# The sixteen transposes of K in one run, into the gram's banks, ahead of the third projection's last tile

## The reference

```
z_l = h @ W_lang.T ; z_g = h @ W_grav.T ; v = h @ W_V.T
A_l = max(zn @ zn.T, 0) * not_eye                  # zn: rows of z_l, each of unit length
A_g = exp(-max(|z_g i - z_g j|^2, 0) / (2 sigma^2)) * not_eye
K   = w_l * row_normalised(A_l * mask) + (1 - w_l) * row_normalised(A_g * mask)
x   = layernorm(x + (K @ v) @ W_O.T)
```

## Time and profile before

| | us |
|---|---|
| median of 3 runs | 1019.85 (1018.96 to 1020.45) |
| span of the profiled execution, first to last instruction | 1016.6 |
| TensorE busy | 1002.1 |
| VectorE busy | 646.2 |
| ScalarE busy | 322.4 |
| GpSimd busy | 151.8 |

### The profile page before, as it was taken

How to read it: one execution, slowest core, us unless ns; L and a number is a source line. 1 busy time by engine, 2 the same in 40 slices (tenths; PEclk the granted TensorE clock), 3 DMA queues, 4 the chain that set the end, 5 groups by cost and what they waited for, 6 DMA issues and landing times.

```text
span 1016.6 us, 15123 instructions
## 1 busy us (share of the span) xinstructions
PE 1002.1 (99%) x5194; PEld 867.0 (85%) x5194; DVE 646.2 (64%) x1786; ACT 322.4 (32%) x632; POOL 151.8 (15%) x155
## 2 busy tenths in 40 slices
PE   9999999999999999999999999999999999999997
PEld 7788888888888888888888889888898888888885
DVE  4565757657485674757757586574856748477488
ACT  4333233232422333233232332324233232242341
POOL 1202111021200212102021100212001121010231
PEclk9999999999999999999999999999999999999999
DMA  8320130403104040140401304031040401403001
GB/s 218 72 43 1 46 80 5 121 0 94 31 21 104 0 117 7 42 84 0 124 0 59 66 11 113 0 97 28 21 103 0 114 11 42 83 0 125 1 21 63
DMA packets 155378, 55.04 MB, mean 54 GB/s; under 512 B 133824, under 2 KB 137920, under 8 KB 155328
## 3 DMA queue, kind: packets, MB, share of 16 engines
q1 hardware_dynamic: 153216, 53.49, 20.9%
q10 hardware_dynamic: 2112, 1.05, 0.4%
HBM read 37.75 MB, written 16.78 MB: 54 GB/s over the span
## 4 chain that ended last, share of the span: by engine, by line
issue 66%; PE 20%; POOL 11%; DVE 2%; POOLq 0%; DMA 0%; ACT 0%; DVEq 0%
POOL mask_r L1014 6%; PE ring L283 5%; PE ring L285 5%; PE ring L284 4%; POOL rstd L1021 3%; PE g_bank L283 2%; PE g_bank L285 2%; PE g_bank L284 2%; POOL r L1008 1%; PE g_bank L278 1%; PE ring L278 1%; POOL u_odd_lo L996 1%; PE g_bank L321 0%; DMA y<-in_x_dram 0%; DVE al L823 0%
## 5 line engine op out<-in xcount | busy, mean ns | idle before, releaser
L660 DVE TENSOR_TENSOR zl_lo<-ring,zl_hi 128x512 fp32r<-128x512 f32 x64 | 44.1, 691 | 117.3 <-ACT zl_hi L525 117.3
L569 ACT ACTIVATE off<-g_bank 128x128 f32<-128x128 f32 (+1 forms) x128 | 40.4, 331 | 227.8 <-DVE diag_out L736 227.3
L1021 POOL TENSOR_TENSOR rstd<-var_eps,neg_half 128x1 f32<-128x1 f32 x64 | 46.0, 719 | 410.2 <-DVE var_eps L855 410.2
L283 PE MATMUL ring<-xT_hi,wgT_hi 128*128 128x512 f32 x256 | 101.6, 397 | 0.0
L283 PE MATMUL ring<-xT_hi,wlT_hi 128*128 128x512 f32 x256 | 101.4, 396 | 0.0
L283 PE MATMUL ring<-wvo_hi,xT_hi 128*128 128x512 f32 x256 | 101.0, 395 | 0.0
L285 PE MATMUL ring<-xT_hi,wlT_lo 128*128 128x512 f32 x256 | 99.9, 390 | 0.0
L285 PE MATMUL ring<-wvo_hi,xT_lo 128*128 128x512 f32 x256 | 99.8, 390 | 0.0
L285 PE MATMUL ring<-xT_hi,wgT_lo 128*128 128x512 f32 x256 | 99.8, 390 | 0.0
L284 PE MATMUL ring<-xT_lo,wgT_hi 128*128 128x512 f32 x256 | 99.8, 390 | 0.0
L284 PE MATMUL ring<-xT_lo,wlT_hi 128*128 128x512 f32 x256 | 99.8, 390 | 0.0
(11 more groups left out here) (121 smaller groups left out, 2248.8 us busy)
## 6 DMA issues: line engine op xcount, KB each, us to landing
xb<-in_x_dram SPq DMA_DIRECT2D x60, 256.0 KB, 4.7
out_dram<-y SPq DMA_DIRECT2D x60, 256.0 KB, 2.0
y<-in_x_dram SPq DMA_DIRECT2D x14, 1024.0 KB, 5.7
y<-in_x_dram SPq DMA_DIRECT2D x4, 256.0 KB, 5.3
al<-in_L_gnn_W_grav_dram ACTq DMA_DIRECT2D x4, 256.0 KB, 5.9
ag<-in_L_gnn_W_lang_dram SPq DMA_DIRECT2D x1, 1024.0 KB, 9.8
xb<-in_L_gnn_W_V_dram SPq DMA_DIRECT2D x1, 1024.0 KB, 11.9
mask_r<-in_L_gnn_W_O_dram SPq DMA_DIRECT2D x4, 256.0 KB, 9.1
```

What stands on the lines that cost most here:

```text
L283: nc.tensor.matmul(psum, lh, rh, start=k == 0, stop=False)
L569: nc.scalar.activation(off[:, mine[0]:mine[-1] + 1, :], g_bank[i][:, j0 * P:(j0 + len(mine)) * P] .rearrange("p (c n) -> p c n", n=P), ACT ...
L660: nc.vector.tensor_tensor(pair[1][:, i, :], bank[:, :], pair[0][:, i, :].bitcast(F32), ALU.subtract).then_inc(evacuated, 1)
L1021: nc.gpsimd.tensor_tensor(rstd[:, i:i + 1], var_eps[:, i:i + 1], neg_half[:, 0:1], ALU.pow)\
```

## The change

Inside the main loop, the four `transpose_k` calls become one, `transpose_whole_k`: sixteen transposes in a row ahead of `u` tile 3, written to the four gram banks, which the masked `zl` gram has left by then. They wait for `k_ready` row tile by row tile and for no ring bank. The four K tiles leave the ring's order, so a batch has 18 tiles in it and not 22. ACT and DVE take the four high and low parts right behind one another, from the gram banks, with three semaphores of their own (`kT_turned`, `kT_hi_written`, `kT_split`); `aggregate` waits for `kT_split`. On DVE the four `lo_k` stand between `u` tiles 2 and 3, `x_transpose(b + 2, 0)` moves from before `lo` of `u` tile 3 to behind it, and the two `lo` of K that stood between `row_sums` and `statistics` of the first two `out` tiles are gone. On ACT the two high parts of K that stood between those of the input are gone too. `last_two` keeps its order.

```diff
@@ -61,8 +32,8 @@
 
 
 BATCH = ([("zg", 1, 0), ("hsq", 0, 0), ("zg", 1, 1), ("zg", 1, 2), ("zg", 1, 3), ("zl", 1, 0), ("r", 0, 0),
-          ("zl", 1, 1), ("zl", 1, 2), ("zl", 1, 3), ("u", 1, 0), ("u", 1, 1), ("u", 1, 2), ("kT", 0, 0),
-          ("u", 1, 3), ("kT", 0, 1), ("out", 0, 0), ("kT", 0, 2), ("out", 0, 1), ("kT", 0, 3), ("out", 0, 2),
+          ("zl", 1, 1), ("zl", 1, 2), ("zl", 1, 3), ("u", 1, 0), ("u", 1, 1), ("u", 1, 2),
+          ("u", 1, 3), ("out", 0, 0), ("out", 0, 1), ("out", 0, 2),
           ("out", 0, 3)])
 
 LAST = (BATCH[:10]
@@ -71,6 +42,7 @@
            ("out", 0, 3), ("kT", 1, 1), ("out", 1, 0), ("kT", 1, 2), ("out", 1, 1), ("kT", 1, 3), ("out", 1, 2),
            ("out", 1, 3)])
 SPLIT = ("zg", "zl", "u", "kT")
+assert len(BATCH) % 2 == 0
 
 
 def splits(tiles):
@@ -200,6 +172,8 @@
         deg_step = sem("deg_step")
         DEG_G, DEG_ALL = 3, 7
 
+        kT_turned, kT_hi_written, kT_split = sem("kT_turned"), sem("kT_hi_written"), sem("kT_split")
+
         bn_written, moments, var_ready, rstd_ready, y_done = (
             sem("bn_written"), sem("moments"), sem("var_ready"), sem("rstd_ready"), sem("y_done"))
 
@@ -432,10 +406,19 @@
                     pe.wait_ge(k_ready, (self.b + db) * T + (i + 1))
                     transposed(bank, [al[:, i, j * P:(j + 1) * P] for j in range(T)]).then_inc(stream_ready, 1)
 
+                def transpose_whole_k(self):
+
+                    for i in range(T):
+                        pe.wait_ge(k_ready, self.b * T + (i + 1))
+                        transposed(g_bank[i], [al[:, i, j * P:(j + 1) * P] for j in range(T)]).then_inc(kT_turned, 1)
+
                 def aggregate(self, db, i, parity):
 
                     bank = self.begin(("out", db, i))
-                    pe.wait_ge(evacuated, self.stream.upto(("kT", db, i)))
+                    if ("kT", db, i) in self.stream.place:
+                        pe.wait_ge(evacuated, self.stream.upto(("kT", db, i)))
+                    else:
+                        pe.wait_ge(kT_split, self.b * T + (i + 1))
                     kT_i = [t[:, i, :].rearrange("p (k n) -> p k n", n=P) for t in kT]
                     product(bank[:, :], lambda k: tuple(t[:, k, :] for t in kT_i), whole_row(u[parity]))\
                         .then_inc(stream_ready, 1)
@@ -456,13 +439,10 @@
                     s.project("zl", i)
                 for i in range(3):
                     s.project("u", i)
-                s.transpose_k(0, 0)
+                s.transpose_whole_k()
                 s.project("u", 3)
-                s.transpose_k(0, 1)
                 for i in range(T):
                     s.aggregate(0, i, parity)
-                    if i + 2 < T:
-                        s.transpose_k(0, i + 2)
 
             def last_two(b, stream):
                 s = Steps(b, stream)
@@ -560,6 +540,10 @@
                     name = (kind, db, i)
                     split_hi(ring[self.stream.bank(name)], self.stream.upto(name), pair, i)
 
+                def hi_k(self, i):
+                    act.wait_ge(kT_turned, self.b * T + (i + 1))
+                    nc.scalar.activation(kT[0][:, i, :], g_bank[i][:, :], ACT.Copy).then_inc(kT_hi_written, 1)
+
                 def copy_off(self, db, diag_read, done, row_tiles=range(T)):
 
                     for i in row_tiles:
@@ -618,14 +602,12 @@
                 until_zl(s)
                 for i in range(3):
                     s.hi("u", 1, i, u[1 - parity])
-                s.hi("kT", 0, 0, kT)
+                for i in range(T):
+                    s.hi_k(i)
                 s.hi("u", 1, 3, u[1 - parity])
-                s.hi("kT", 0, 1, kT)
 
                 for k in range(T):
                     whole_hi_part(b + 2, k, xT)
-                    if k + 2 < T:
-                        s.hi("kT", 0, k + 2, kT)
 
             def last_two(b, stream):
                 s = Steps(b, stream)
@@ -728,6 +710,11 @@
                 def lo(self, kind, db, i, pair):
                     name = (kind, db, i)
                     split_lo(ring[self.stream.bank(name)], self.stream.split_upto(name), pair, i)
+
+                def lo_k(self, i):
+                    dve.wait_ge(kT_hi_written, self.rows(0, i))
+                    nc.vector.tensor_tensor(kT[1][:, i, :], g_bank[i][:, :], kT[0][:, i, :].bitcast(F32),
+                                            ALU.subtract).then_inc(kT_split, 1)
 
                 def diagonals(self, db, rows_done, factor, col, done, row_tiles=range(T)):
 
@@ -898,18 +885,16 @@
                 s.combine(0, 2)
                 s.combine(0, 3)
                 s.lo("u", 1, 2, u_next)
-                s.lo("kT", 0, 0, kT)
+                for i in range(T):
+                    s.lo_k(i)
+                s.lo("u", 1, 3, u_next)
                 x_transpose(b + 2, 0)
-                s.lo("u", 1, 3, u_next)
-                s.lo("kT", 0, 1, kT)
                 for i in range(T):
                     if i + 1 < T:
                         x_transpose(b + 2, i + 1)
                     whole_lo_part(b + 2, i, xT)
                     s.residual(0, i)
                     s.row_sums(0, i)
-                    if i + 2 < T:
-                        s.lo("kT", 0, i + 2, kT)
                     s.statistics(0, i)
                     if i:
                         s.normalise(0, i - 1)
```

## The result

The changed kernel takes 1021.30 us (median of 17 runs, 1020.63 to 1022.62) against 1019.66 for the kernel before, measured beside it (17 runs, 1018.52 to 1020.45). The ratio of the two is 1.0021, 95% interval 1.0014 to 1.0028: slower, by about as much as a measurement of this kernel can tell. The profiled execution took 1020.85, with a span of 1018.9; the span before was 1016.6.

A forecast was written before the change was run, and what follows sets the result against it. TensorE, 99% busy, bounds the kernel; at a return VectorE's last instruction of the old batch times it. Six returns x 0.56 lost minus 8 x 0.12 gained, +2.40 on 1019.85, gives 1022.25 us; its own range 1020.9 to 1024.4.

The forecast's parts named there:

- TensorE's part: K stage: one run of sixteen transposes, priced from the kernel's start, gains 0.12 us a batch; bounds nothing to 0.17.
- VectorE's part: Last `normalise`, counted from the start of the K stage: 1.33 + 0.63 - 0.60 - 0.80 = 0.56 us later; bounds 0.40 to 0.75.
- the other three terms: VectorE: `x_transpose` 0 behind `lo`, 0.63 later; second `lo` of K gone, 0.60 earlier; third and fourth gone, 0.80 earlier.
- The two small gaps that I set equal: VectorE: `whole_lo_part` 0 waits for ScalarE's copy; the wait before the first residual, 0.74 against 0.65, goes; taken to cancel.
- Where it costs: At six returns the mirror comes 0.56 us later; elsewhere nothing, third diagonal ready at 369.99 before its gram row at 370.14.
- The sum: Whole kernel: six returns lose 3.36 us, eight K stages gain 0.96, net +2.40; range +1.0 to +4.5.
- the 3.25 us between the median and the span: Added to the forecast span of 1019.0 as the median's excess over the profiled span, giving 1022.25 us.
- VectorE's lateness reached TensorE: Rival at returns: lateness does not reach TensorE, only 14 x 0.12 = 1.7 less stands, 1018.15 us; chance 0.17.
- The second stop: Rival at returns: VectorE's 1.56 us stop amid the diagonals moves, up to 9.4 us either way, 1013 or 1032; chance 0.07.
- VectorE did not catch up: Rival: VectorE catches up, its end comes a microsecond earlier, the returns' 5.2 us go, 1013.0 us; chance 0.10.
- the run did not wait for `combine`: Rival in the K stage: the last `combine` becomes late, 17 us lost, 1037; chance 0.04 together with the clock.
- the clock stayed at 1.00: Rival: the longer run lowers the clock, `u` tile 3 at half clock, 38 us, 1058; chance 0.04 together with `combine`.

The follow-up runs named there:

- the run with four runs in the new banks: Changed kernel with its gram banks and semaphores, but four runs of four transposes and ScalarE's and VectorE's order of before; one run, 1019.95 us beside 1020.10.
- the written-out kernels: Both kernels with the loop of seven turns written out, no returns: kernel before 1014.65 us, ratio 0.9948; changed kernel 1012.91 us, ratio 0.9929.
- the reordered one: Changed kernel, two block transposes ahead of `lo` of `u` tile 3, VectorE's other input work spread; 1013.02 us with the loop (ratio 0.9935), 1012.97 written out.

## Why the prediction was right

- *TensorE's part.* Forecast 0.12 us a batch from the start's run of sixteen; measured 0.15 in the K stage (15.52 to 15.37) and 0.13 in a whole batch (61.21 to 61.08). The twin at the start was a good price, and the run with four runs in the new banks shows that its length is what counts.
- *VectorE's part.* The sum of four terms was 0.56; measured 20.02 to 20.04 for 19.47. `lo` of `u` tile 3 came at 5.32 from K where 5.35 was forecast, and from there to the last `normalise` it was 307.33 - 292.63 = 14.70 for 306.21 - 290.76 = 15.45: 0.75 less, where the other three terms say 0.77. The two small gaps that I set equal nearly are: `whole_lo_part` 0 starts 0.11 after the transposes ahead of it end (293.24 + 1.29 to 294.64), and the wait before the first residual is gone.
- *Where it costs.* Six returns, and no other place: shown by the written-out kernels, where the same lateness costs nothing, and by the reordered one, where the returns cost nothing because VectorE is early. At the other boundary the cover of 0.91 shrank to 0.19; the forecast of 369.99 against 370.14 had said 0.15.
- *The sum.* Forecast +2.40; the ratio of the runs says 2.1 (1.4 to 2.9), the spans differ by 2.3, the medians by 1.64. In the traces the loop became 2.6 us longer: the six batches behind a return lost 3.7 together, where 3.36 was forecast, and the eight others gained 1.0, where 0.96 was. What I took as constant is the stretch from the last `normalise` to the mirror, and it is not: over the six returns it was 6.13 to 6.91 before and 6.30 to 6.92 after, 0.26 more in sum. Both stops of VectorE's stream vary, the first from 2.58 to 3.10, the second from 1.49 to 1.81.
- *The level, and luck.* I called the 3.25 us between the median and the span start and end outside the span. That is wrong: wherever a run's time and span are both on record they differ by 1.7 to 1.95. The rest is that the times lie in two groups (last section): the profiled execution belongs to the first, the median of three runs to the second. So 1022.25 was a forecast for the second group, whose median is 1022.28; the median of all, 1021.30, is the last run of the first one, which has nine of the 17. Group against group the change costs 1.9 us and 2.3. The direction does not hang on this; how near the number came does.
- *The rivals.* VectorE's lateness reached TensorE, whose weights waited 10.6 us at the mirror for 6.1, some 0.75 more at each return. The second stop stayed at the same place in the diagonals. VectorE did not catch up, the run did not wait for `combine` (286.02 + 1.41 = 287.43, and no wait shows in a run begun at 287.31, whose last four transposes come 1.3 later), and the clock stayed at 1.00 through the run. The Trainium skill ("TensorE: Matmul & The Clock Gate", Part 4) says that transposes don't count as TensorE activity the way matmuls do; in this case a run of 1.9 us among matmuls brought no fall of the clock.

What I would not call shown: why VectorE's stream stops twice after a return. The written-out loop shows that the return is the condition; what happens in the engine stays open.

## What to carry to other kernels

When an engine is 99% busy, look for the few places where it is not, find which engine's last instruction times each, and judge an edit by that instruction: here 0.13 us gained in eight batches was outweighed by 0.56 and more lost in the six others, by an engine that is idle a third of the time. A loop's return can be such a place, and then either the order ahead of it is worth tuning or the loop is worth writing out. Before work is grouped for one engine, see which waits of the others the ungrouped order had been filling.

## What was not expected

The times of the two kernels lie in two groups each, 1.2 to 1.5 us apart; the changed kernel's 17 runs are nine from 1020.63 to 1021.30 and eight from 1021.99 to 1022.62, with nothing between, and the kernel before has eight up to 1019.09 and nine from 1019.66. The changed kernel's runs of the first group have a mean granted clock of 0.999 or 1.000, those of the second 0.996 to 0.998. The profiles say where it falls. TensorE has one wait of 2 us in the start of every kernel here, for the low part of a transposed weight, 1.97 to 2.05 in the eleven profiles. Behind it the clock is granted in full in five of them, whose mean clock is 0.999 or 1.000, and in half for a few microseconds in the six others. The wait in the kernel before written out and in the changed kernel written out, then windows (length, busy, clock) of the first and of the second:

```profile
32.45 0.49 PE L283 MATMUL ring<-kT_hi,u_odd_hi 128*128 128x512 f32 x1 [2.01 <-DVE kT_lo L674]
```

```profile
32.47 0.47 PE L257 MATMUL ring<-kT_hi,u_odd_hi 128*128 128x512 f32 x1 [2.01 <-DVE kT_lo L656]
```

```profile
30.00:32.00 2.00, 0.44 (x2) 1.00 0.62 98
32.00:34.00 2.00, 1.55 (x4) 0.69 1.11 175
34.00:36.00 2.00, 2.00 (x6) 0.50 1.07 168
36.00:38.00 2.00, 2.00 (x9) 0.96 0.53 83
```

```profile
30.00:32.00 2.00, 0.45 (x3) 1.00 0.65 103
32.00:34.00 2.00, 1.53 (x7) 1.00 1.14 179
34.00:36.00 2.00, 2.00 (x11) 1.00 0.99 157
```

The wait is the same, 2.01 us in both; the level after it is 0.50, the lower one of 1.2 GHz, in one and 1.00 in the other. In the first the loop's first batch begins at 58.65, in the second at 57.06; in all profiles it is 57.1 to 57.4 where the clock stays and 58.4 to 58.9 where it falls. Why it falls in one execution and not in another is not shown. So up to 0.15% between two medians of this kernel can be a matter of how many of their runs fell into which group. The account above rests on batches and K stages of the traces, which lie behind this wait; the medians and ratios do not escape it.
